# Seven graph poolings of a GNN on one core: nine of 49 destination blocks gathered instead of seven, and the first row stores issued by ScalarE

## What is computed

```python
agg = jax.ops.segment_sum(h[src], dst, num_segments=N)      # sum over incoming edges
# sage, four layers: h = relu(h @ W_self[l] + (agg / max(deg, 1)) @ W_neigh[l] + bias[l]), none on the last
# plain, once: agg of the normalised rows, used by the node update
# conv, two layers: h = elu((A + I) @ (d * h) @ W * d + b), d = deg ** -0.5
```

## Time and profile before

| what | value |
| --- | --- |
| median of 3 runs | 3296.05 us (3292.64 to 3297.19) |
| profiled execution | 3296.43 us, span 3294.9 us |
| mean granted TensorE clock | 0.961 |
| busy | PE 89%, DVE 32%, ACT 22%, POOL 34% |
| sage chain | 1231.7 to 2265.6 us |
| plain chain | 2334.6 to 2578 us |
| conv chain | 2765.4 to the end |

### The profile page before, as it was taken

The page is one execution under the profiler, slowest core; times in us unless marked ns, Lnnn a source line. Parts: engine busy times, 40 slices in busy tenths (PEclk is TensorE's granted clock), DMA queues, the critical chain, the costliest instruction groups (busy, mean ns, idle before and its releaser), DMA issues. The chain is left out here.

```text
span 3294.9 us, 44136 instructions
## 1 busy us (share of the span) xinstructions
PE 2945.9 (89%) x18657; PEld 1743.1 (53%) x18657; DVE 1044.3 (32%) x1858; ACT 734.1 (22%) x1172; POOL 1116.3 (34%) x1012
## 2 busy tenths in 40 slices
PE   1799869996799869999999999998799767999998
PEld 1688735553444335555555555553455664555554
DVE  5999822222200261111111111114111463222122
ACT  4799811222200240000000000001000373111000
POOL 5000023330000004653562662662366001553564
PEclk9999989998899989999999999999899987999999
DMA  7244599993367226666666665662766203665665
GB/s 256 62 133 133 157 229 163 179 149 85 94 148 157 51 65 205 181 170 170 180 166 166 180 177 166 175 175 54 195 181 173 56 34 106 173 180 162 169 173 153
DMA packets 768367, 492.61 MB, mean 150 GB/s; under 512 B 362500, under 2 KB 749836, under 8 KB 767568
## 3 DMA queue, kind: packets, MB, share of 16 engines
q1 hardware_dynamic: 705362, 395.76, 49.1%
q0 software_dynamic: 30112, 62.69, 6.8%
q10 hardware_dynamic: 32702, 31.44, 3.2%
HBM read 334.89 MB, written 76.82 MB: 125 GB/s over the span
## 5 line engine op out<-in xcount | busy, mean ns | idle before, releaser
L2134 PE MATMUL acc<-tbuf,hs 128*128 128x448 fp8e4 x8232 | 1600.3, 353 | 26.4 <-PEq L1226 13.0
L2111 POOL DMA_INDIRECT grow<-hrows,glist x882 | 942.6, 1069 | 792.9 <-PE acc L2158 395.1
L2134 PEld LDWEIGHTS acc<-tbuf,hs 128*128 128x128 f16 x8232 | 800.4, 98 | 769.2 <-issue 58.0
L2273 DVE TENSOR_TENSOR edge_loc<-iota,gdl 128x768 f16<-128x768 bf16 x147 | 140.5, 971 | 763.0 <-PE acc L2158 617.0
L711 ACT ACTIVATE stage<-quad 128x784 fp8e4<-128x784 f32 x392 | 290.4, 827 | 7.8 <-PE quad L731 5.3
L731 PE MATMUL quad<-K,S 128*128 128x196 bf16 x1568 | 277.0, 249 | 15.6 <-DVE K L655 10.2
L1605 PE MATMUL acc<-tbuf,hs 128*128 128x512 fp8e4 (+1 forms) x1300 | 281.7, 370 | 8.9 <-DMA tbuf<-table 8.9
L735 PE MATMUL deg<-K,S 128*128 128x196 bf16 x1568 | 275.8, 247 | 0.0
L1484 PE MATMUL acc<-tbuf,hs 128*128 128x512 fp8e4 (+1 forms) x1300 | 266.3, 368 | 0.7 <-issue 0.7
L2242 ACT ACTIVATE H<-B,vectors 128x448 f32<-128x448 f32 (+2 forms) x56 | 37.4, 668 | 808.5 <-DVE B L2313 538.2
L1484 PEld LDWEIGHTS acc<-tbuf,hs 128*128 128x128 f16 x1300 | 123.4, 98 | 143.5 <-issue 2.9
(11 more groups left out here) (300 smaller groups left out, 1989.8 us busy)
## 6 DMA issues: line engine op xcount, KB each, us to landing
tbuf<-table SPq DMA_DIRECT2D x294, 448.0 KB
tbuf<-table SPq DMA_DIRECT2D x294, 336.0 KB
table<-stage SPq DMA_DIRECT2D x6, 5488.0 KB
grow<-hrows,glist POOLq DMA_INDIRECT x882
hrows<-hs SPq DMA_DIRECT2D x28, 448.0 KB
feat<-in_edge_attr_dram ACTq DMA_DIRECT2D x27, 448.0 KB, 5.3
C<-factors ACTq DMA_DIRECT2D x2, 3136.0 KB, 12.4
table<-stage SPq DMA_DIRECT2D x2, 2744.0 KB
```

Source lines behind the costliest of these rows:

```text
L2111: g.indirect_dma_start(out=grow[:, n % 2, t, :], out_offset=None, in_=k.hrows[l % 2], in_offset=bass.IndirectOffsetOnAxis(k.glist[:, i // ...
L2134: mm = T.matmul(acc(s, h), rows[l % 2][:, g * US + r, part, :], counts[:, (r - lo) * STRIP + h * HALF:(r - lo) * STRIP + (h + 1) * HALF], ...
L2273: V.tensor_tensor(hot[:, n % 2, :, :], k.iota[:, 0:P].unsqueeze(1).to_broadcast([P, GH, P]), k.gdl[:, i // GU, i % GU * GH:(i % GU + 1) * ...
```

## The change

Nine blocks are gathered, in groups of 4, 4 and 1, which are banks, turns and stores of their own (parts 6, 7 and 8). The 40 dense blocks are six strips, four of seven blocks and two of six (halves of 384 columns). 27 units are placed by `UNITS_AT`, the first behind (0,10), the last behind (5,6); four strips have a unit behind piece 13. DVE's program is written by piece as TensorE's is: behind each unit, the comparison of the unit after next; `leave_bank` of a strip after all of these. Sources, ring and the 14 pieces per strip stay. ScalarE issues the four first row stores of sage and plain at the head of the chain's block, and then, without the wait for five used pieces, the load of `C`; SP no longer stores in `split_rows`. Semaphores count chunks by `ORDER` instead of halves.

```diff
+STRIP_BLOCKS = [7, 7, 7, 7, 6, 6]
+GROUPS = [4, 4, 1]
+NG = sum(GROUPS)
-GB0 = (NU - 1) * US
+GB0 = sum(STRIP_BLOCKS)
...
-NGH = GU * US
+NGH = GU * NG
...
-def load_piece(k, sp, tbuf, s, i, slot=None):
+def load_piece(k, sp, tbuf, s, i, slot=None, strips=None):
...
-    sp.dma_start(tbuf[:, at:at + (hi - lo) * SU].rearrange("p (b u) -> p b u", u=SU),
-                 k.table[t * US + lo:t * US + hi, :, bass.ds(s * SU, SU)].rearrange("b l u -> l b u")
+    start, n = (s * SU, SU) if strips is None else (sum(strips[:s]) * P // 2, strips[s] * P // 2)
+    sp.dma_start(tbuf[:, at:at + (hi - lo) * n].rearrange("p (b u) -> p b u", u=n),
+                 k.table[t * US + lo:t * US + hi, :, bass.ds(start, n)].rearrange("b l u -> l b u")
...
@@ split_rows, SyncE
-            for a, b in ROW_STORES if store else ():
-                sp.wait_ge(lo_ok.h, lo_ok.at(b))
-                store_rows(k, sp, k.hs, 0, 4 * a, min(4 * b, NS))
...
-TURN_AT, TURN_LAST_AT, OWN_AT = 2, 12, 12
-GATHER_AT = {at: n for n, at in enumerate(sorted([(s, i) for s in range(1, DENSE) for i in (1, 4, 7, 10)] + [(4, 13)]))}
+DENSE = len(STRIP_BLOCKS)
+PART_BLOCKS = STRIP_BLOCKS + GROUPS
+ORDER = [(0, 0), (0, 1), (1, 0), (1, 1), (6, 0), (2, 0), (2, 1), (3, 0), (3, 1), (4, 0), (4, 1), (7, 0), (8, 0), (5, 0),
+         (5, 1)]
+TURN_AT, OWN_AT = 2, 12
+PART_TURNS = {(2, 12): 6, (5, 5): 7, (5, 12): 8}
+UNITS_AT = [[10, 13], [1, 3, 6, 8, 11, 13], [3, 4, 6, 9, 13], [0, 3, 4, 7, 10, 13], [0, 3, 6, 9], [0, 1, 3, 6]]
+GATHER_AT = {at: n for n, at in enumerate((s, i) for s, places in enumerate(UNITS_AT) for i in places)}
+PART_DONE = {GU * sum(GROUPS[:i + 1]) - 1: DENSE + i for i in range(len(GROUPS))}
...
@@ layer_chain, SyncE: when the rows of a strip or part are stored
+                    for s in range(DENSE):
+                        stores[(l * DENSE + s + 1) * NH + TURN_AT + R + 2] = (l, s)
+                    for (s, i), part in PART_TURNS.items():
+                        stores[(l * DENSE + s) * NH + i + R + 2] = (l, part)
...
@@ layer_chain, TensorE, dense_piece
-                                              counts[:, (r - lo) * STRIP + h * HALF:(r - lo) * STRIP + (h + 1) * HALF],
+                                              counts[:, (r - lo) * strip + h * half:(r - lo) * strip + (h + 1) * half],
...
@@ layer_chain, ScalarE
+                if not conv:
+                    for r0, r1 in ROW_STORES:
+                        store_rows(k, act, k.hs, 0, 4 * r0, min(4 * r1, NS))
                 if factor is not None:
-                    act.wait_ge(used.h, used.at(R))
                     act.dma_start(k.C[:, :], k.factors[factor:factor + 1, :].to_broadcast([P, NP])).then_inc(row_in.h, 16)
...
@@ layer_chain, VectorE
+                hots(0, 0)
+                hots(0, 1)
                 for l in range(L):
                     for s in range(DENSE):
-                        for e in events(l, s)[0:1]:
-                            if e[1] != LAST_S:
-                                turned_in(*e)
-                        for h in units(s)[2:] + units(s + 1)[:2]:
-                            hots(l, h)
...
+                        for i in range(NH):
+                            if i == TURN_AT and (l or s):
+                                turned_in(*strip_before(l, s))
+                            if (s, i) in PART_TURNS:
+                                turned_in(l, PART_TURNS[s, i])
+                            if (s, i) in GATHER_AT:
+                                u = GATHER_AT[s, i]
+                                if u in PART_DONE:
+                                    leave_bank(l, PART_DONE[u], 0)
+                                    if conv:
+                                        finish(l, PART_DONE[u], 0)
+                                n = l * NGH + u + 2
+                                if n < L * NGH:
+                                    hots(n // NGH, n % NGH)
+                        for q in range(2):
+                            leave_bank(l, s, q)
```

More of the change, by code:

```diff
@@ L687, in _ @@
                 dve.wait_ge(g_step.h, g_step.at(2))
-                mine, after = (blocks[:, GB0 % 4 + i:GB0 % 4 + i + US] for i in range(2))
+                mine, after = (blocks[:, i:i + NG] for i in range(2))
                 V.tensor_tensor(excess[:, :], after, mine, ALU.subtract).then_inc(g_step.h, 1)
@@ L1067, in _ @@
                 flat = k.edge_pairs.rearrange("(a b) t -> a (b t)", b=P)
-                for n in range(US):
+                for n in range(NG):
                     nc.gpsimd.indirect_dma_start(out=k.glist[:, n, :], out_offset=None, in_=flat,
@@ L1205, in store_rows, with split_rows @@
                  rows[:, b0:b1, :, :].rearrange("p b a f -> p b (a f)")).then_inc(k.sem("hr_out").h, 16)
-def split_rows(k, v, over_src, at, weight, own, tbuf, keep, store=False):
+def split_rows(k, v, over_src, at, weight, own, tbuf, keep):
     nc = k.nc
@@ L2019, in layer_chain @@
     R = k.ring
-    total, turns = L * DENSE * NH, (L - 1) * NU
+    total, turns, parts = L * DENSE * NH, (L - 1) * len(ORDER), len(PART_BLOCKS)
     sage, conv = kind == "sage", kind == "conv"
@@ L2029, in layer_chain @@
     g_got = [k.sem(f"g_got{b}", fresh=True) for b in range(2)]
[L2030 removed]
+    spans = {s: (GU * sum(GROUPS[:s - DENSE]), GU * sum(GROUPS[:s - DENSE + 1])) for s in range(DENSE, parts)}
     def count(l, s, q):
[L2034 removed]
+        return l * len(ORDER) + ORDER.index((s, q)) + 1
     def before(l, s, q):
[L2038 removed]
+        same = [(m, c[0]) for m in range(L) for c in ORDER if c[1] == q]
         i = same.index((l, s))
@@ L2086, in _ @@
[L2086 to L2092, removed]
+                        sp.wait_ge(z_lo.h, z_lo.at(count(l, s, chunks_of(s)[-1])))
@@ new lines, in _ @@
+                        store_rows(k, sp, rows[(l + 1) % 2], (l + 1) % 2, PART_AT[s], PART_AT[s] + PART_BLOCKS[s])
+                for s, q in ORDER if conv else ():
+                    if q != chunks_of(s)[-1]:
+                        continue
+                    b0, b1 = PART_AT[s], PART_AT[s] + PART_BLOCKS[s]
+                    sp.wait_ge(o_copied.h, o_copied.at(count(0, s, q)))
+                    if b1 < NS:
+                        sp.dma_start(out[b0 * P:b1 * P, :].rearrange("(b p) f -> p b f", p=P), out_rows[:, b0:b1, :]
+                                     ).then_inc(o_out.h, 16)
+                    else:
+                        assert b1 - b0 == 1
+                        sp.dma_start(out[b0 * P:N, :], out_rows[0:N - b0 * P, b0, :]).then_inc(o_out.h, 16)
@@ L2178, in turn @@
                         return
-                    pe.wait_ge(ready.h, ready.at(count(l, s, 1)))
-                    for q in range(2):
-                        if leaves and j > turns:
-                            pe.wait_ge(o_copied.h, o_copied.at(2 * (j - turns - 1) + q + 1))
-                        elif j:
-                            pe.wait_ge(z_lo.h, z_lo.at(2 * (j - 1) + q + 1))
+                    pe.wait_ge(ready.h, ready.at(count(l, s, chunks_of(s)[-1])))
+                    for q in chunks_of(s):
+                        last = before(l, s, q)
+                        if last is not None and last > turns:
+                            pe.wait_ge(o_copied.h, o_copied.at(last - turns))
+                        elif last is not None:
+                            pe.wait_ge(z_lo.h, z_lo.at(last))
                         for i, b in enumerate(blocks_of(s, q)):
```

158 lines of the change are left out of this document (68 added, 90 removed).

## The result

The changed kernel takes **3347.3 us** (3346.4 to 3348.8, 4 runs) beside 3296.4 (3292.6 to 3297.2, 4 runs) of the kernel before: 1.0151 of it, 95% interval 1.0138 to 1.0164. The forecast was 3346.0. The profiled span grew from 3294.9 to 3344.8 us.

The account below looks back on a forecast made before the run. The prediction took TensorE's own instruction stream to bound the kernel. Its terms, -73.3 + 28.1 + 42.8 + 53.7 - 9.6 + 3.1 + 5.1 = +49.9 us, on 3296.4 gave 3346, range 3292 to 3402.

Parts of the forecast that it names:

- Dense columns: TensorE's dense matmuls: two strips per pooling narrow from 448 to 384 columns, 0.189 to 0.162 us a matmul; -73.3 us.
- Units: TensorE's gathered matmuls: six more units per pooling, 42 in all, at 0.67 us each; +28.1 us.
- Strip ends: Units behind piece 13: TensorE waits while DVE compares before reading the finished strip; 21 more times 2.04 us, +42.8.
- Waits for gathered rows: All seven poolings: TensorE waits where GpSimd's gather DMAs cannot keep up with the units; +53.7 us.
- the walk: Unit-by-unit reckoning of each pooling: a unit starts when its piece is done or its data landed; gave the gathered-row waits.
- That the two stand for each other: Strip-end and gathered-row waits: without the former, the latter grow 42.6 us and the sum falls only 14.5.
- Row stores: Start of plain: with stores on ScalarE the chain starts 7.6 us earlier, plus 2 for the clock; -9.6 us.
- Sage's start: Sage's first pooling: C loads behind the stores, unit 0 waits 6 us, replacing a table-piece wait of 2.93; +3.1.
- Clock: TensorE after strip-end waits: a lower granted clock costs 1.7 us at one boundary in seven, 21 more boundaries; +5.1.
- Rival (b): Gather keeps pace: GpSimd's rows come in time, waits shrink to some 3 us, 3284 us in all; chance 0.08.
- Rival (c): Slow landing: gathers share DMA engines with table pieces, waits are 136.6 us, 3429 us in all; chance 0.12.

Follow-up runs that it names:

- e1: The changed kernel, but DVE reads a finished strip ahead of the comparison for the unit behind piece 13: 3331.9 us, 1.0094 of the kernel before.
- e2: The kernel before, with DVE reading a finished strip ahead of the comparison for the unit behind piece 13: 3283.8 us, 0.9958 of the kernel before.
- e3: The changed kernel with three of the six gather DMAs of each unit left out: 3286.4 us, 0.9960 of the kernel before.
- e12: The kernel of e3 again, on another chip (4): 3285.5 us, 0.9964 of the kernel before.
- e6: The kernel before with its four row stores on ScalarE, the load of C keeping its wait: 3292.9 us, 0.9967 of the kernel before.
- e5: The changed kernel with the row stores back on SP and the load of C behind its old wait: 3547.9 us, 1.0742 of the kernel before.
- e10: The changed kernel, unedited, as a control on chip 12: 3553.9 us, 1.0693 of the kernel before.
- e4b: The changed kernel with each gather DMA fetching rows of 256 bytes in place of 512: 3525.5 us, 1.0662 of the kernel before.

## Why the prediction was right

The mechanism held in every large term, and each term came within about 5 us. That the sum came within 1.3 us is luck: the errors cancel, and the four runs of e1 alone lie 19 us apart. By the steps of its sum:

- **Dense columns**, -73.3 from 0.189 and 0.162 us a matmul. 28 matmuls of 448 columns last 1287.67 - 1282.37 = 5.30 us in e1, 0.189. Sixteen of 384 columns in the kernel after, 1735.27 - 1732.66 = 2.61, 0.163:

```profile
1732.66 2.76 PE L2152 MATMUL acc<-tbuf,hs 128*128 128x384 fp8e4 x16
1735.27 1.50 PE L2210 MATMUL acc<-weights,H 128*128 128x128 f32 x12
```

  By the line through 128 and 448 columns the step was right without a row of 384. Measured -71 to -73.
- **Units**, +28.1. 0.67 us each still: start to start, where no wait follows, 56 ns a matmul in both kernels, so +28.6.
- **Strip ends**, 21 x 2.04 = +42.8. 28 of them now, 1.90 each: +40. The mechanism (comparison before reading) is shown by e1 and e2.
- **Waits for gathered rows**, +53.7: 51.0 of idle time, 58.5 with the 47 tails of 0.16, shown to be the supply's by e3 and e12. By pooling 5.5, 5.1, 6.6, 8.8, 14.6 (plain), 4.7, 5.6, forecast 5.3, 4.6, 4.6, 10.7, 18.6, 3.9, 6.0. The places held: (2,6) waits in all seven poolings, 9.6 us together, (5,3) 8.3 and (3,4) 5.8; (5,6), 6.7, the prediction does not name. Its inputs held too: landing after the last DMA's end 1.63 to 4.13 us, median 2.3 (taken: 2.2, from the nearest row); stretch 0.24 back to back and 0.71 behind a wait for a free buffer (0.27 and 0.6); first gather of plain 18.5 after its start (20). The longest single wait is 2.2, where the walk had one of 3.3: they are spread over 47 places. (The sum for plain that is written as 239.5 adds up to 239.8; nothing else changes by it.)
- **That the two stand for each other** ("if the boundaries cost nothing, the walk gives 42.6 us more of these waits and a sum only 14.5 lower"): e1 took 15.4 off, with 29.0 more of waits. The net was right; the exchange was 29.0 for 48.7 (the prediction: 42.6 for 57), and 8.2 us of the gain went into the dense matmuls, which are busy for 1543.7 us in e1 and 1535.5 in the kernel after.
- **Row stores**, -9.6: -8.4 from the end of sage to the start of plain, and the 2 us for the clock were there as well, 2.3 in the first matmuls of the chain; e6 has -9.5 in all. The chain starts 0.3 after DVE, not 1.0.
- **Sage's start**, +3.1 as a wait of 6 at unit 0. The size is near, +2.3, the place is wrong. Nothing waits at (0,10) in sage's first pooling; the wait for a table piece of the earlier trace rows grew instead, from 2.93:

```profile
1256.91 9.99 PE L2152 MATMUL acc<-tbuf,hs 128*128 128x448 fp8e4 x44 [5.20 <-DMA tbuf<-table]
1266.74 0.83 PE L2178 MATMUL acc<-edge_loc,grow 128*128 128x128 f16 x12
```

  I took the stores and the load of `C` to leave table pieces alone, and the piece came later than before; by 1266.7 the comparison was done. In e5, with both given back, the same wait is 3.72, and 5.06 in e10.
- **Clock**, +5.1: dense matmuls that run slow behind a wait lose about 1 to 1.7 us each (2443.73 above), 6.8 us in five places. The kernel before has 5.3 in three, of which 2.2 at the start of plain belong to the row stores; so the term is +3.7. The mechanism was incomplete: not only strip ends do it, a wait for rows does as well (2.19 us at 2188.48, with no strip end near), which the step left out. Its size came out because it was small; in e1, with no strip-end waits and 80 us of waits for rows, it is 15.1 us in ten places.

Rival (b), gather keeps pace, is what e3 makes by force (3286; it gave 3284). Rival (c), slow landing, had 5.1 us after the last DMA; no waited unit of the kernel after needed more than 4.13.

What the forecast did not have at all is the other chip: it priced the kernel without asking where it runs. Where it was first timed it held to 1.3 us; on chip 12 the same kernel was 207 us slower, and none of the rows of before points to it.

## What to carry to other kernels

When work moves from the bound engine to one that feeds it, take the feeder's pitch (here 7.8 to 8.1 us a unit), lay the units further apart than that (7.4 to 9 us left 33.9 us of waits, 9 us left 0.9), and walk them one by one: the average load (GpSimd 41% busy) says nothing, and one line of places was worth 59 us. In an engine's program, put what releases the bound engine before what prepares the unit after next. Two waits that stand behind each other are not added up: take one away and the other grows, so price a repair with the second still there.

## What the runs showed of the hardware

The kernel before took 3296 to 3302 us in five groups of runs (chips 1, 4, 5 and 11 among them) and 3322 in a sixth, on chip 12; the kernel after took 3347 where it was first timed and 3554 on chip 12, with 90.7 us of unnamed stops of TensorE; why is open. A comparison of DVE (128x768, 0.96 us) lengthens an indirect DMA of GpSimd that starts in it from 1.00 to 1.60 us; with 4 columns the effect is gone (0.02 us a unit). Rows of 256 bytes in place of 512 leave the mean DMA as it is (1064 ns in e4b, 1066 in e10) and land 0.2 to 0.35 us sooner (e4b against e10 and e5). After waits of about 2 us, the granted clock fell from 1.00 to 0.57 over 4 us, and the matmuls behind them lost 1 to 1.7 us each time.
